# Sums of squares of expert weights: TensorE's gram diagonal in place of ScalarE's square

## What is computed

```python
x = x + xattn(layernorm(x), ctx, W_k, b_k, gamma, beta)   # sim -> layernorm -> softmax
x = x + ffn(layernorm(x), Wg, W1, W2, W3)
# ffn: scores = x @ Wg.T; top 2 of E = 8 experts, softmax of the two
#   h = silu(x @ W1[e].T) * (x @ W2[e].T);  y += w[..., e] * (h @ W3[e].T),  H = 352
```

## Time and profile before

| | us |
|---|---|
| median of 3 runs | 431.38 (429.61 to 434.36) |
| profiled execution | 432.07 |
| its span, first to last instruction | 430.3 |
| TensorE matmuls busy | 354.9 (82%) |
| VectorE busy | 273.9 (64%) |
| ScalarE busy | 266.8 (62%) |
| GpSimd busy | 212.2 (49%) |

### The profile page before, as it was taken

The page is one execution under the profiler, slowest core; times in us unless marked ns, Lnnn a source line. Parts: engine busy times, 40 slices in busy tenths (PEclk is TensorE's granted clock), DMA queues, the critical chain, the costliest instruction groups (busy, mean ns, idle before and its releaser), DMA issues.

```text
span 430.3 us, 8658 instructions
## 1 busy us (share of the span) xinstructions
PE 354.9 (82%) x2023; PEld 230.2 (54%) x2024; DVE 273.9 (64%) x734; ACT 266.8 (62%) x458; POOL 212.2 (49%) x338
## 2 busy tenths in 40 slices
PE   2866489479486608899999999999999999999980
PEld 0432364365365505466666666666666666666640
DVE  1165767778798592666766766676676667667640
ACT  2378667767787491566666566666666656666640
POOL 1126536436456133355565565556556556655531
PEclk9998757868855558999999999999999999999995
DMA  7947564765656751134543544454454455445422
GB/s 236 418 194 232 221 214 159 289 208 163 220 192 211 230 222 51 50 61 89 95 70 80 98 75 77 93 94 66 85 98 74 76 94 86 72 87 94 79 34 40
DMA packets 21809, 57.28 MB, mean 133 GB/s; under 512 B 4832, under 2 KB 4960, under 8 KB 20256
## 3 DMA queue, kind: packets, MB, share of 16 engines
q0 software_dynamic: 8736, 20.53, 27.4%
q1 hardware_dynamic: 13056, 36.56, 24.8%
HBM read 38.17 MB, written 18.91 MB: 133 GB/s over the span
## 4 chain that ended last, share of the span: by engine, by line
PE 55%; DVE 4%; DMA 3%; issue 1%; POOL 1%; POOLq 0%; ACT 0%; DVEq 0%; ACTq 0%
PE bank L1072 31%; PE bank L1102 17%; PE bank L1063 4%; PE bank L1087 3%; DMA x_s<-n_table,gcol 2%; DVE stage L840 2%; DMA out<-kvj_s,scol 1%; POOLq L65 0%; POOL w3rs L485 0%; PE bank L1040 0%; DVE stage L836 0%; POOL gcol L468 0%; DVEq L890 0%; DVE kvg_s L882 0%; ACT kvj_s L631 0%
## 5 line engine op out<-in xcount | busy, mean ns | idle before, releaser
L873 DVE SCALAR_TENSOR_TENSOR stage<-W,w3sc,stage 128x512 f16<-128x512 f16 x117 | 84.1, 746 | 6.8 <-ACT stage L604 6.8
L1102 PE MATMUL bank<-stage,n_s 128*128 128x512 f16 (+1 forms) x351 | 82.2, 379 | 1.5 <-issue 1.5
L604 ACT ACTIVATE stage<-W,w3sc 128x512 f16 x117 | 79.5, 717 | 0.0
L1072 PE MATMUL bank<-Wp,kvg_s 128*128 x480 | 78.0, 312 | 0.2 <-issue 0.2
L1072 PE MATMUL bank<-Wp,kv_s 128*128 x456 | 74.2, 312 | 0.0
L1072 PEld LDWEIGHTS bank<-Wp,kvg_s 128*128 128x128 f16 x480 | 46.7, 97 | 25.8 <-issue 4.1
L901 DVE TENSOR_TENSOR n_s<-bank,n_s 128x384 f16<-128x384 f32 x39 | 21.7, 557 | 59.7 <-ACT n_s L620 59.7
L1072 PEld LDWEIGHTS bank<-Wp,kv_s 128*128 128x128 f16 x456 | 44.5, 98 | 24.2
L470 POOL DMA_INDIRECT x_s<-n_table,gcol x39 | 50.4, 1293 | 6.8 <-issue 5.1
L1102 PEld LDWEIGHTS bank<-stage,n_s 128*128 128x128 f16 (+1 forms) x351 | 34.2, 98 | 34.5 <-issue 1.7
L616 ACT ACTIVATE L_s<-bank,winv 128x352 f32<-128x352 f32 x39 | 21.6, 553 | 45.0 <-PE bank L1072 41.4
(11 more groups left out here) (161 smaller groups left out, 586.1 us busy)
## 6 DMA issues: line engine op xcount, KB each, us to landing
W<-in_w SPq DMA_DIRECT2D x8, 1408.0 KB, 7.3
W<-in_w SPq DMA_DIRECT2D x8, 768.0 KB, 5.9
stage<-in_xT SPq DMA_DIRECT2D x4, 1024.0 KB, 6.5
x_s<-in_x SPq DMA_DIRECT2D x16, 256.0 KB, 6.2
out<-x_s SPq DMA_DIRECT2D x16, 256.0 KB, 4.3
n_table<-n_s SPq DMA_DIRECT2D x16, 256.0 KB, 2.7
stage<-in_ctxT SPq DMA_DIRECT2D x1, 768.0 KB, 8.2
x_s<-n_table,gcol POOLq DMA_INDIRECT x39
```

The costliest lines, as they stand in the source:

```text
L604: eng.activation(w3p[r][:, c * D:(c + 1) * D], W3[:, bass.ds(e * W3N + c * D, D)], ACT.Copy, scale=w3sc[:, bass.ds(e, 1)]).then_inc(s_w3h, 1)
L873: eng.scalar_tensor_tensor(w3p[r][:, W3N + c * D:W3N + (c + 1) * D], W3[:, bass.ds(e * W3N + c * D, D)], w3sc[:, bass.ds(e, 1)], w3p[r][:, ...
L1072: mm = eng.matmul(bank[2 * which + r][:, 0:H], n_, w_, start=(c == 0 and k == 0), stop=(c == DC - 1 and k == 2))
L1102: mm = eng.matmul(bank[4 if r else 7][:, :], h_, w_, start=(c == 0 and k == 0), stop=(c == HC - 1 and k == 2))
```

## The change

TensorE takes the sums of squares. A bf16 view of the fp32 weights, every second 16-bit word, is the upper half of each fp32 word, so the value cut to bf16. For each 128 columns TensorE multiplies this block with itself (stationary and moving operand are the same) and adds 11 such products in PSUM: the diagonal holds the sums of squares over the partitions. Both halves of an expert lie side by side in bank 7. VectorE multiplies both with the identity and sums each row (`weight_squares`), and one matmul of ones gives the sum to all partitions. ScalarE's `squares` is gone, and VectorE's small reduce (L702) with it.

The grams of expert 0 stand ahead of TensorE's loop and its masked sum ahead of VectorE's loop. The others stand in TensorE's slots n = 0 to 13, expert n // 2 + 1, half n % 2, behind the norms and ahead of the scores; the masked sum stands at the end of VectorE's slot of odd n.

```diff
-            def squares(k, h):
-                eng.wait_ge(s_w[k % RING], 16 * (k // RING + 1))
-                wait(eng, s_wqp, k - 1)
-                wait(eng, s_wq, 2 * k + h)
-                eng.activation(wjunk, wst[k % RING][:, h * WH:(h + 1) * WH], ACT.Square,
-                               accum_out=wsq[:, k % 2, h:h + 1]).then_inc(s_wq, 1)
...
-                if n // 2 + 1 < E:
-                    squares(n // 2 + 1, n % 2)
...
-            squares(0, 0)
-            squares(0, 1)
             batches(slot, None, weights)
...
+            def weight_squares(k):
+
+                eng.wait_ge(s_wg, 2 * k + 2)
+                wait(eng, s_wqp, k - 1)
+                wait(eng, s_wq, k)
+                eng.tensor_tensor_reduce(wjunk[:, :, :], bank[7][:, 2 * P:4 * P].rearrange("p (h m) -> p h m", m=P),
+                                         ident[:, None, :].to_broadcast([P, 2, P]), 1.0, 0.0, ALU.mult, ALU.add,
+                                         wsq[:, k % 2:k % 2 + 1]).then_inc(s_wq, 1)
+
             def weight_sums(k):
                 eng.wait_ge(s_wqp, k + 1)
+                eng.wait_ge(s_wg, min(2 * k + 3, 2 * E))
                 wait(eng, s_wrs, k - 1)
                 cols = slice(k % 2, k % 2 + 1)
-                eng.tensor_reduce(wsum[:, cols], bank[7][:, E:E + 2], AX.X, ALU.add).then_inc(s_wsum, 1)
-                eng.wait_ge(s_wsum, k + 1)
-                eng.tensor_tensor(wsum[:, cols], wsum[:, cols], guard[:, 0:1], ALU.max).then_inc(s_wmax, 1)
+                eng.tensor_tensor(wsum[:, cols], bank[7][:, E:E + 1], guard[:, 0:1], ALU.max).then_inc(s_wmax, 1)
...
                 if n % 2 == 0 and 0 <= n // 2 < E:
                     weight_sums(n // 2)
+                if n % 2 == 1 and 0 < n // 2 + 1 < E:
+                    weight_squares(n // 2 + 1)
...
             gram_copy(0)
+            eng.wait_ge(s_const, NCONST)
+            weight_squares(0)
 
             batches(slot)
...
                 wait(eng, s_sc, n - 3 if n > 4 else 0)
-                eng.wait_ge(s_wq, 2 * k + 2)
-                eng.matmul(bank[7][:, E:E + 2], ones[:, :], wsq[:, k % 2, :], start=True, stop=True).then_inc(s_wqp, 1)
+                eng.wait_ge(s_wq, k + 1)
+                eng.matmul(bank[7][:, E:E + 1], ones[:, :], wsq[:, k % 2:k % 2 + 1], start=True, stop=True).then_inc(s_wqp, 1)
+
+            def weight_gram(k, h):
+
+                eng.wait_ge(s_w[k % RING], 16 * (k // RING + 1))
+                wait(eng, s_wq, k)
+                pairs = wst[k % RING].bitcast(BF16).rearrange("p (n two) -> p n two", two=2)
+                for c in range(h * WH // P, (h + 1) * WH // P):
+                    cols = pairs[:, c * P:(c + 1) * P, 1]
+                    mm = eng.matmul(bank[7][:, (2 + h) * P:(3 + h) * P], cols, cols, start=(c == h * WH // P),
+                                    stop=(c == (h + 1) * WH // P - 1))
+                mm.then_inc(s_wg, 1)
...
                 if n % 2 == 1 and 0 <= n // 2 < E:
-                    eng.wait_ge(s_wsum, n // 2 + 1)
+                    eng.wait_ge(s_wmax, n // 2 + 1)
+                if n >= 0 and n // 2 + 1 < E:
+                    wait(eng, s_sc, n - 3 if n > 4 else 0)
+                    weight_gram(n // 2 + 1, n % 2)
...
             sims(0, 0)
+            weight_gram(0, 0)
+            weight_gram(0, 1)
             eng.wait_ge(s_cin, 16 * 2)
```

More of the change, by code:

```diff
@@ L83, in build @@
         ctx_s = stage[:, DC * N:DC * N + T]
-        wjunk = stage[:, DC * N + T:DC * N + T + WH // 2].bitcast(BF16)
+        wjunk = stage[:, DC * N + T:DC * N + T + P].bitcast(BF16).rearrange("p (h m) -> p h m", m=P)
         wk_s = sb("wk_s", [P, C])
@@ L117, in build @@
         guard = sb("guard", [P, E])
-        wsq = sb("wsq", [P, 2, 2])
+        wsq = sb("wsq", [P, 2])
         wsum = sb("wsum", [P, 2])
@@ L204, in build @@
         s_w3 = [sem(f"s_w3_{i}") for i in range(E)]
-        s_wq, s_wqp, s_wsum, s_wmax, s_wrs, s_wsc, s_wrec, s_winv = [
-            sem(n) for n in ("s_wq", "s_wqp", "s_wsum", "s_wmax", "s_wrs", "s_wsc", "s_wrec", "s_winv")]
+        s_wg, s_wq, s_wqp, s_wmax, s_wrs, s_wsc, s_wrec, s_winv = [
+            sem(n) for n in ("s_wg", "s_wq", "s_wqp", "s_wmax", "s_wrs", "s_wsc", "s_wrec", "s_winv")]
         s_hi, s_lo = sem("s_hi"), sem("s_lo")
```

## The result

The changed kernel takes 454.77 us (452.27 to 455.71), the kernel before 432.87 in the same runs: ratio 1.0506, interval 1.0422 to 1.059, so 5% slower, 22 us. The forecast was 448, with a range of 437 to 457. The profiled execution has a span of 452.3 us, 22.0 more than before.

What follows compares the result with a forecast made beforehand. No engine is full from 22 to 142 us; chains between engines set the pace. Start +3.9 up to load 4, with load stalls +14.3 by g12's scores, plus 1.7 for the clock: +16 in total, 448 us, range 437 to 457.

Steps and rivals of the forecast that it cites:

- The wait that decides: TensorE's first gram in n = 6, 8, 10, 12 waits for late weight loads, holding everything behind it; forecast 444 to 454, chance 0.70.
- The gain of ScalarE lost: Sixteen squares, 21.9 us, leave ScalarE, 14 of them in the loop; the gain is lost in TensorE's wait for loads.
- The prices: Masked sum on VectorE about 425 ns plus 80 ns accumulator read; gram pair on TensorE 54 ns, 108 at half clock.
- rival D: Strided 16-bit operands cost what fp32 ones do, each gram on the path 0.6 to 1.1 us more: +7, 455; chance 0.12.
- The start: Ahead of the loop: VectorE's first product +2.8 us, keys' evacuation +3.5; slots carry +3.9 up to load 4.
- the term of the clock: Half clock after stalls in n = 8 and 12, 3.7 and 2.0 us later; a quarter to a half taken, +1.7.
- L4: Landing time of weight load 4 in the changed kernel: 65.3 + 3.9 = 69.2 us.
- L4 to L5: Landing of load 4 to landing of load 5: half-clock grams, scores to transposes, nT to issue, landing; 18.6 us.
- L5 to L6: Landing of load 5 to landing of load 6: grams, scores to keys' end, keys' evacuation to issue, landing; 20.2 us.
- L6 to L7: Landing of load 6 to landing of load 7: same as from load 4 to load 5, 18.6 us.
- B: Rival: grams fill TensorE's gaps in the loop and keep its clock up, so +16 becomes +5, 437; chance 0.10.
- C: Rival: ScalarE was the bound; its relief gives 4 to 6 us, 426, if loads land before TensorE arrives; chance 0.08.

Runs made afterwards that it cites:

- the kernel with other data: Changed kernel whose first half-grams of experts 4 to 7 multiply the previous expert's buffer, already landed, so the work stays without the load wait: 431.94 us, ratio 0.9993.
- its neighbour: Changed kernel with loads 4 to 7 issued early and expert 0's grams and masked sum moved behind the first product: 432.3 us, ratio 1.0002.
- The fillers: Changed kernel with 50 useless matmul pairs of 128 columns ahead of the grams in n = 8 and 12: 449.86 us, ratio 1.0419.
- the kernel before with fillers: Kernel before with 80 useless matmul pairs of 128 columns at the end of TensorE's slots n = 4, 8 and 12: 431.03 us, ratio 0.9958.

## Why the prediction was right

*The wait that decides: right.* The four stalls came in n = 6, 8, 10 and 12, 18.4 us in all. Shown from both sides: without them the loss is nothing, they alone make 15 of 22 us, and two independent ways of having the load in time take 21 of the 22 us away.

*The gain of ScalarE lost: right, and for a further reason.* Even where nothing stalls, of 19 us 5 to 6 come through. In the kernel with other data VectorE's queue has no gap in the late slots (order of time):

```profile
119.49 0.42 DVE L692 CUSTOM_DVE_ANT_1 stage<-bank,ident 128x256 bf16<-128x256 f32 x1
119.84 0.08 DVE L692 DVE_READ_ACCUMULATOR2_ANT wsq<- 128x1 f32 x1
119.84 0.69 DVE L656 BATCH_NORM_STATS2 bn<-x_s 128x6 f32<-128x512 f32 x1
...
120.91 0.68 DVE L737 CUSTOM_DVE_ANT_0 L_s<-L_s,beta_s 128x512 f32<-128x512 f32 x1
...
122.58 1.67 DVE L722 SCALAR_TENSOR_TENSOR Wp<-W,wscale,Wp 128x1408 f16<-128x1408 f32 x1
```

and ScalarE waits 7.0 us for VectorE's minimum from 60 to 135 us. But it waits 7.4 us there for GpSimd's alpha (L403) too, so the rows don't say which of the two holds the rest back, and no run tested it.

*The prices: right.* Masked sum 424 ns for 425. A gram pair, from the rows of eleven: 0.79 and 1.33 us, less a latency near 0.2, over 10 steps 0.06 and 0.11 us, for 0.054 and 0.108. The dearer price that the prediction names from the Trainium skill (TensorE: Matmul & The Clock Gate, Back-to-back issue gap), 81 ns a pair, did not show: 22 pairs took 1.42 us at 21.22, clock 1.00, where by an estimate from that figure it would be 1.8. Operands that take every second 16-bit word cost nothing more, so rival D is out.

*The start: right in size.* The product came 3.0 us later (2.8 forecast), the keys' evacuation 3.6 (3.5), and TensorE's sums over the product, ahead of the keys, waited 1.3 us for it. But which of the two carries the start into the loop I left open. The run that brought only the product forward gained nothing; the one that brought the keys forward too came out 0.6% lower than its neighbour (0.9944 for 1.0002, with intervals that overlap). That points to the keys.

*The sum: short by 7 us, 4 of them in the term of the clock.* By the marks in the profiled execution, forecast and found: L4 69.2 and 71.09; L4 to L5 18.6 and 18.96; L5 to L6 20.2 and 23.77; L6 to L7 18.6 and 19.25; to the scores of n = 13 4.6 and 6.68. I had worked out 3.7 for half clock in n = 8 and 2.0 in n = 12, and the intervals came out 3.6 and 2.1 longer: the whole of both, where the prediction, in its words, took "a quarter to a half of it: +1.7". That is 4 of the 7 us. It rested on a stall of "only some 1.5 to 2 us"; the stalls were 3.35 and 4.15, since I had bounded TensorE's own arrival by adding to an interval that held waits. The fillers show that the clock is the cause and what it is worth there: with it up, the two stretches took 20.4 and 3.8 us, where I had 20.2 and 4.6 without it.

Another 1.9 is L4, and this is not a price of the change. In this execution the clock fell in n = 4: the squares of the batch at 45.72 took 1.70 us for 0.95 at 42.88 in the kernel before, and ScalarE then waited 3.5 us for the keys. The kernels with fillers, unchanged up to there, had it the other way round: in the kernel before it fell (first row), in the changed kernel it stayed up (second row), and the grams of n = 6 began at 69.69, 0.5 from the forecast.

```profile
43.45 1.71 PE L960 MATMUL bank<-ones,prod_s 128*128 128x1 f32 x8
46.33 1.05 PE L961 MATMUL bank<-ones,prod_s 128*128 128x1 f32 x8
```

From these squares to the issue of load 4 it is 15.4 us up and 17.9 down in the kernel before, 16.5 up and 18.6 down in the changed one. So the clock differs here from execution to execution of the same instructions, and that is worth 2.1 to 2.5 us. Over all profiled executions these squares ran low in 4 of 8 with the grams and in 3 of 5 without. A sum that starts from the marks of one profile carries this error, and here the profile before happened to be one without the fall. The last 1 us is spread over the two other stretches.

*The rivals.* B asked for gaps that shrink. In their place came waits for loads, and the clock in the loop was 0.72, before 0.73. The Trainium skill (TensorE: Matmul & The Clock Gate, Loop structure matters more than you think) has it that a wait for a DMA between matmuls loses the clock; the trace agrees in n = 8 and 12, where it was 1.00 ahead of the stalls and 0.50 behind them. C's ceiling of 4 to 6 us for ScalarE's relief was about what the run without squares gave, 4.6 to 5.6, but the loads came too late for it.

## What to carry to other kernels

Moving work to an engine with free time moves its waits too: look at where in the new engine's queue the wait stands, who is behind it, and when the data arrive. Where the data are late, either issue the load earlier or let the new engine read them a slot later; here each took back 21 of the 22 us, and an early load gained nothing in the kernel whose reader stood last anyway. When a stall on the path is on TensorE and the clock was up ahead of it, price the work behind it at half clock in full, and get the length of the stall from its own steps, not from an interval that already holds waits. And look at the clock in a second profile before its marks go into a sum to the microsecond.

## What the runs showed of the hardware

Fillers of no use, 50 pairs of 128 columns in each of two stalls, made the kernel 4 to 5 us faster. In n = 8 TensorE's granted clock stayed at its upper level, 2.4 GHz, through the load's wait and the slot behind it (1.00 from 85.10 to 92.40 us). Without them it was at its lower level, 1.2 GHz, behind the stall of 3.35 us (0.50 from 90.05 to 97.40).

Being busy did not always keep it up: in n = 12 the fillers kept TensorE busy without a gap, and the clock was still 0.50 from 125.5 to 128.2 us, then 0.99 from 128.2 to 134.0. Why it fell there, no run shows.

A stationary and a moving operand that are the same strided 16-bit view of fp32 words ran at 0.06 us a pair of 128 by 128, as dense fp16 did (80 dense pairs took 4.79 us at 51.56 in the kernel before with fillers, at a clock of 0.97).
